# Layer 0's scores of batches 2 to 7: four heads in one block on TensorE, the second pair of heads in two other PSUM banks

## What is computed

```python
gk = k.reshape(B, G, KV_HEADS, N, D_HEAD).mean(axis=1)
gv = v.reshape(B, G, KV_HEADS, N, D_HEAD).mean(axis=1)
scores = jnp.einsum('bghnd,bhsd->bhns', gq, gk)
scores = scores + gbias
attn = jax.nn.softmax(scores.astype(jnp.float32), axis=-1)
out = jnp.einsum('bhns,bhsd->bhnd', attn, gv)
```

## Time and profile before

| what | value |
|---|---|
| three executions | 761.25, 761.84 (median), 762.82 us |
| the profiled execution | 761.44 us |
| its span, first to last instruction | 759.5 us |
| PE busy | 738.1 us, 97% of the span |
| DVE busy | 555.8 us, 73% |
| ACT busy | 383.1 us, 50% |
| POOL busy | 187.2 us, 25% |
| TensorE clock granted, mean | 0.998 of full speed |

### The profile page before, as it was taken

The page is one execution under the profiler, slowest core; times in us unless marked ns, Lnnn a source line. Parts: engine busy times, 40 slices in busy tenths (PEclk is TensorE's granted clock), DMA queues, the critical chain, the costliest instruction groups (busy, mean ns, idle before and its releaser), DMA issues.

```text
span 759.5 us, 16816 instructions
## 1 busy us (share of the span) xinstructions
PE 738.1 (97%) x6559; PEld 556.0 (73%) x6559; DVE 555.8 (73%) x1642; ACT 383.1 (50%) x1063; POOL 187.2 (25%) x235
## 2 busy tenths in 40 slices
PE   7899999999999999999999999999998999999996
PEld 5565757775787578657865786588576878999996
DVE  4878875869776877688678867787859764255997
ACT  3755557356535654555456545642561436554422
POOL 0235212153116311540154025304210422000000
PEclk9999999999999999999999999999999999999999
DMA  7950020402040204020402030213204304000000
GB/s 226 377 142 1 4 82 2 111 1 58 3 111 1 58 2 112 2 56 7 109 1 57 19 96 6 53 31 83 57 2 107 118 3 111 1 1 1 15 22 22
DMA packets 55702, 43.07 MB, mean 57 GB/s; under 512 B 37900, under 2 KB 48804, under 8 KB 54216
## 3 DMA queue, kind: packets, MB, share of 16 engines
q1 hardware_dynamic: 55624, 42.01, 20.8%
HBM read 32.42 MB, written 9.58 MB: 55 GB/s over the span
## 4 chain that ended last, share of the span: by engine, by line
PE 83%; DVE 11%; ACT 2%; DMA 1%; issue 1%; POOL 1%; SPq 0%; DVEq 0%; ACTq 0%
PE ps L1753 15%; PE ps L1836 14%; PE ps L1896 7%; PE ps L2059 4%; PE ps L2037 4%; PE ps L1739 4%; PE ps L2006 4%; PE ps L1761 4%; PE ps L1787 3%; PE ps L1848 3%; PE ps L1774 3%; DVE shared L1482 2%; DVE shared L1475 2%; PE ps L1703 2%; PE ps L1919 2%; PE ps L1931 2%
## 5 line engine op out<-in xcount | busy, mean ns | idle before, releaser
L1753 PE MATMUL ps<-veF,hB 128*128 128x512 f32 x256 | 121.6, 606 | 0.0
L1301 DVE COPY_PREDICATED shared<-ghot,ps 128x512 f32<-128x512 int32 x128 | 88.2, 727 | 3.4 <-PE ps L1753 0.6
L848 ACT ACTIVATE sc<-sc,nmax 128x128 f32<-128x128 f32 (+1 forms) x128 | 57.1, 447 | 58.4 <-DVE nmax L1287 58.4
L1753 PEld LDWEIGHTS ps<-veF,hB 128*128 128x128 f32 x256 | 45.2, 189 | 49.4 <-issue 40.2
L648 POOL TENSOR_TENSOR sc<-sc,rg 128x384 f32<-128x384 f32 x64 | 51.6, 827 | 70.0 <-DVE rg L1274 70.0
L1836 PE MATMUL ps<-early_masks,oeF 128*128 128x256 f32 x256 | 63.5, 386 | 2.7 <-DVE wide L1331 1.6
L705 POOL TENSOR_TENSOR ve<-mv,eps 128x2 f32<-128x2 f32 x24 | 8.6, 357 | 233.3 <-DVE mv L1187 233.3
L1836 PE MATMUL ps<-wide,oeF 128*128 128x256 f32 x256 | 62.3, 386 | 0.0
L1896 PE MATMUL ps<-hC,early 128*64 128x128 f32 x1024 | 61.7, 275 | 0.2
L2037 PE MATMUL ps<-hE,veF 128*128 128x256 f32 x256 | 59.5, 382 | 0.3 <-ACT wide L957 0.3
L1896 PEld LDWEIGHTS ps<-hC,early 128*64 128x64 f32 x1024 | 55.7, 137 | 5.4 <-ACT wide L886 2.5
(11 more groups left out here) (253 smaller groups left out, 1527.5 us busy)
## 6 DMA issues: line engine op xcount, KB each, us to landing
chosen<-hot_scratch SPq DMA_DIRECT2D x16, 512.0 KB, 5.8
v_scratch<-shared SPq DMA_DIRECT2D x16, 512.0 KB, 5.3
vg<-v_scratch SPq DMA_DIRECT2D x16, 512.0 KB, 5.4
veF<-in_L_ffn_value_experts SPq DMA_DIRECT2D x1, 2048.0 KB, 9.9
oeF<-in_L_ffn_output_experts SPq DMA_DIRECT2D x1, 2048.0 KB, 16.0
early<-in_L_attn_w_qkv SPq DMA_DIRECT2D x1, 1536.0 KB, 16.6
shared<-bias_scratch SPq DMA_DIRECT2D x2, 512.0 KB, 6.2
veF<-in_L_ffn_W SPq DMA_DIRECT2D x1, 1024.0 KB, 5.3
```

The costliest lines, as they stand in the source:

```text
L848: act.activation(v, v, ACT.Exp, bias=nmax[:, h % RING, t:t + 1], scale=-1.0, accum_out=denB[:, h * T + t:h * T + t + 1]).then_inc(s_("f_e" ...
L1301: dve.copy_predicated(val[:, t, :].rearrange("p (h k) -> p h k", h=HF), ghot[:, t * HF:(t + 1) * HF, e].bitcast(I32).unsqueeze(2) .broadca ...
L1753: pe.matmul(ps[:, vbank(j), :], tok(hB, t), veF[:, :].rearrange("p (h e k) -> p e h k", h=HF, e=EF)[:, e, :, :], start=True, stop=True).th ...
```

## The change

For batches 2 to 7 PE now makes the scores of all four heads at place 1, directly behind chunk 1 of the products, in one block of eight matmuls. The first pair stays in banks 4 and 6, the second goes to banks 7 and 1. The wait for DVE's reading of the first pair (`a_sc`) is gone; each pair still raises `a_s`. The turned scores, until now in banks 1 and 2, go to banks 2 and 4. The code of DVE, ACT and POOL stands in the same order as before, DVE's S1 still at place 4; only the bank numbers in it differ. Batches 0 and 1 are as they were.

```diff
         def logits_bank0(b, p, hp):
             if b == 1 and p == 1:
                 return 1 + hp
-            return (4 + p if early_batch(b) else 4) + 2 * hp
+            if early_batch(b):
+                return 4 + p + 2 * hp
+            return ((4, 6), (7, 1))[p][hp]
 
         def turned_bank0(b, hp):
-            return 5 + 2 * hp if early_batch(b) else 1 + hp
+            return 5 + 2 * hp if early_batch(b) else 2 + 2 * hp
...
-                if n in (S0, S1):
-                    p = (S0, S1).index(n)
-                    if p == 0:
+                if n == S0 or n == S1 and early_batch(b):
+                    if n == S0:
                         wait_apart(pe, (s_("a_qs"), b + 1), (s_("a_ks"), b + 1))
...
-                    elif not early_batch(b):
-                        pe.wait_ge(s_("a_sc"), b * 8 + 4)
-                    for t in range(T):
-                        for hp in range(2):
-                            mm = pe.matmul(ps[:, logits_bank0(b, p, hp), t * N:(t + 1) * N],
-                                           qT[head_rows(hp), p, t * P:(t + 1) * P], kT[head_rows(hp), p, :],
-                                           start=True, stop=True)
-                    mm.then_inc(s_("a_s"), 1)
+
+                    for p in ((S0, S1).index(n),) if early_batch(b) else range(2):
+                        for t in range(T):
+                            for hp in range(2):
+                                mm = pe.matmul(ps[:, logits_bank0(b, p, hp), t * N:(t + 1) * N],
+                                               qT[head_rows(hp), p, t * P:(t + 1) * P], kT[head_rows(hp), p, :],
+                                               start=True, stop=True)
+                        mm.then_inc(s_("a_s"), 1)
```

## The result

The changed kernel is slower. Its median is 762.51 us (12 runs, 761.62 to 763.35) beside 761.55 us for the kernel before (12 runs, 759.95 to 762.82): ratio 1.0017, 95% interval 1.0009 to 1.0024, so 0.7 to 1.8 us more time (the two medians by themselves are 0.96 us apart). The forecast was 2.1 us less.

A forecast was written before the change was run, and what follows sets the result against it. PE was taken as the bound; gains of 0.16 (batch 2), 0.39 (batch 3) and 4 x 0.38 (batches 4 to 7) sum to 2.07 us, giving 759.8 us, own range 759.2 to 760.4, full range 758.8 to 761.8.

The forecast's parts named there:

- What bounds the kernel, and the join: PE bounds batches 3 to 7; joining two blocks of four score matmuls saves 0.39 us of PE's time a batch.
- The estimate of 0.33: Score blocks: two drains of TensorE less a batch, worth 0.33 us by the skill's page; the prediction stayed with the rows.
- Batch 2: At T0 the removed wait comes back as one for POOL; of 1.00 us gain, 0.16 is left.
- the 1 us that I had named as a sign: Batch 2: about 1 us of PE's idle time before or within T0, for POOL's line 640.
- Batch 3: No tail of layer 1 beside it, POOL's division just in time for T0: gain 0.39 us.
- DVE's S1 and the norm behind it: Batches 4 to 7: S1 and the normed tile come 0.38 us earlier, PE's wait stays: gain 0.38 each.
- The rival "slower": Batches 4 to 7: chunk 3's delay makes the normed tile 0.87 us later; 2.9 us slower, 764.8; chance 0.06.
- The sign that I named for being wrong: At PE's turning of the normed tile, a wait of over 0.5 us would show the forecast wrong.
- the rival before it: The wait moves to T0 everywhere, PE standing still for POOL's division; about 761.6 us, chance 0.07.

The follow-up runs named there:

- e4_before_pool_more: The kernel before, with one more POOL operation (128x512) behind the two divisions of N0 in batches 4 to 7; 764.13 us, ratio 1.0039.

## Why the prediction was wrong

**What bounds the kernel, and the join.** Right. PE's own work was the bound; the block of eight cost 0.87 more than a block of four, 0.39 less than two, in the chain at batch 6 (16 records in 2.00 us, as in batch 0), with the banks 7 and 1 as with batch 0's. The estimate of 0.33 from the Trainium skill's "TensorE: Matmul & The Clock Gate", "Single matmul latency", was low; by batch 3's segment it is 0.40.

**Batch 2.** Right: 0.13 us left of 1.00, forecast 0.16. The removed wait came back as one for POOL's division, in two pieces. The records show 0.51 us of it as idle time, half of the 1 us that I had named as a sign; by the starts 0.87 us came back:

```profile
84.59 0.66 PE L1693 MATMUL ps<-ident,sc 128*128 128x128 f32 x4 [0.17 <-POOL sc L642]
...
85.59 0.66 PE L1693 MATMUL ps<-ident,sc 128*128 128x128 f32 x4 [0.34 <-POOL sc L642]
```

**Batch 3.** Right: 0.40, forecast 0.39.

**DVE's S1 and the norm behind it.** This step failed. It read: "it begins straight after the reciprocal ... 373.80, 0.38 earlier. Behind it in DVE's order stand mask 12 ... the tile 0.38 earlier: the wait stays about what it is." The start of S1 was right: the reciprocal at 373.89 and S1 at 373.98 in a trace that runs 0.18 us later. But the prediction took mask 12's length as fixed, a term that it put at nothing without a reason. It let POOL divide until 376.01 in one paragraph, and moved S1 and with it mask 12 forward in the next, which puts the mask at 375.56 - 0.38 = 375.18. It asked of POOL only who waits for it (rightly no one: T0 began 0.40 us earlier, without a wait), not what runs beside it. Measured from the batch's first score matmul, mask 12 began 0.41 us earlier and took 0.71 us longer, so the addition, the tile and PE's turning of it came 0.30 us later. Each batch lost 0.30 instead of gaining 0.38: 4 x 0.68 = 2.7 us, the term that turned the sign. From -2.07 this gives +0.65. The interval is +0.7 to +1.8, so between nothing and a microsecond more stays unexplained, as in e4_before_pool_more.

**The rival "slower"** had the right victim, the normed tile and PE's wait for it, and the wrong cause and price: it wanted S1 later than 374.18, S1 was earlier (373.98), and it was slower all the same, by about 1 us and not 2.9. Its chance of 0.06 stood for the wrong mechanism, so that "slower" came out is no credit to it. The sign that I named for being wrong (a wait of over 0.5 us at the turned tile) did just show, with 0.51. (A slip in the rival before it changes nothing: 761.84 less batch 2's 0.16 is 761.7, not 761.6.)

**The trace of before had it.** All masks of the kernel before, by the source view of line 1331 (duration ns: min/median/max):

```profile
L1331 DVE TENSOR_TENSOR early_masks<-chosen,oT x64: 657/685/2379, 72.3 to 586.6; 128x512 f32<-128x512 uint8 x64
L1331 DVE TENSOR_TENSOR wide<-chosen,oT x64: 657/685/1391, 77.6 to 590.0; 128x512 f32<-128x512 uint8 x64
```

The longest of the second row stands in batch 2 behind S1, in a run of four masks that takes 3.20 us from 85.25, beside the division of the earlier trace rows that ends at 86.09. The 2379 stands beside POOL here, and PE waited for that very mask:

```profile
71.74 1.90 POOL L606 TENSOR_TENSOR vg<-x,mv 128x1024 f32<-128x1024 f32 x1
73.78 2.16 POOL L609 TENSOR_TENSOR vg<-vg,rstd 128x1024 f32<-128x1024 f32 x1
...
72.28 4.21 DVE L1331 TENSOR_TENSOR early_masks<-chosen,oT 128x512 f32<-128x512 uint8 x2
...
76.54 1.13 PE L1836 MATMUL ps<-early_masks,oeF 128*128 128x256 f32 x4 [1.11 <-DVE early_masks L1331]
```

The two masks end at 76.49, again 0.55 us after POOL (73.78 + 2.16 = 75.94). This is the other row, the 1.1 us that I passed over: PE lost time to the same overlap in the kernel before. A maximum of two and of three times the median was the question to ask. I had written of batch 2 only that DVE is late.

## What to carry to other kernels

When work moves on one engine, lay the new times of all engines over each other, not only the waits between them: an operation on POOL that nobody waits for can still stretch one on DVE that everybody waits for. Before trusting a duration in a sum, look at its maximum beside its median, and find what ran beside the longest. When a block is joined on the bound engine, look for the step that now has the least slack; here moving one short reciprocal into DVE's idle time turned +0.17% into -0.35%, and with the scores beside it -0.48%.

## What the runs showed of the hardware

A mask, a DVE operation with two inputs in SBUF, does not do its work beside a POOL operation that reads SBUF. It starts in the records, and ends 0.54 to 0.55 us after POOL's does. That holds for every mask of over 0.72 us in all eight traces, whatever it overlapped: 0.79 us where POOL's operation had begun 0.80 us ahead of it, 1.12 at 0.47 ahead, 1.40 at 0.19 ahead, 2.38 beside the longer operation of line 609. So the mask waits for POOL's end, and is not merely slower. The whole length counts as busy time, and no view of waits shows it.

It goes the other way too. In the norm behind mask 12 two tiny operations of POOL come up while masks 13 and 14 run (changed kernel, batch 6):

```profile
377.71 1.26 DVE L1333 TENSOR_TENSOR wide<-chosen,oT 128x512 f32<-128x512 uint8 x2
377.87 0.55 POOL L707 TENSOR_TENSOR ve<-mv,eps 128x2 f32<-128x2 f32 x1 [1.70 <-DVE mv L1189]
378.50 1.03 POOL L709 TENSOR_TENSOR rstd<-ve,half 128x2 f32<-128x2 f32 x1
```

Their usual lengths are 0.20 and 0.70 us (medians of 24 each). The 0.68 us more stand on the way to the normed tile in batches 4 to 7, before the change as after it. No run here takes them away.

Operations of DVE of other kinds ran beside POOL at their usual time, in the changed kernel: the scores' pass with one input in PSUM (line 1218, max 426 ns for a median of 419; 27 of 64 beside POOL), the predicated copy out of PSUM (56 of 128), and the reduction with one SBUF input (29 of 32):

```profile
L1218 DVE CUSTOM_DVE_ANT_0 sc<-ps,early x64: 387/419/426, 18.8 to 450.1; 128x256 f32<-128x256 f32 x64
...
L1303 DVE COPY_PREDICATED shared<-ghot,ps x128: 703/729/743, 46.9 to 554.6; 128x512 f32<-128x512 int32 x128
...
L1390 DVE TENSOR_REDUCE max<-wide x32: 649/677/686, 154.2 to 624.5; 128x8 f32<-128x512 f32 x32
```

But the plain multiplication by a scalar from SBUF to SBUF is held up with one input: line 1229 of the kernel before, in the attention of batches 0 and 1, beside POOL's division of the other head. Three of its eight are 1.23 us long and end 0.15 us after POOL.

```profile
L1229 DVE TENSOR_SCALAR sc<-sc,rdenA x8: 341/352/1233, 23.0 to 36.3; 128x256 f32<-128x256 f32 x8
```

The Trainium skill has a rule for this, on the page "SBUF — State Buffer", section "SBUF: two separate sides": DVE and GpSimd share a pair of SBUF ports under an exclusive lock, taken for a whole instruction by whichever starts first, and it counts for DVE operations in a two-port mode, and for those with two SBUF inputs against a GpSimd operation that reads SBUF. The masks of all eight traces agree, and so do the two POOL operations above. Which of the two started first can't be told from the records to the last 0.05 us: the long ones of line 1229 are recorded 0.04 us ahead of POOL's operation, and were held up all the same. By that rule, which I had not weighed, mask 12 would stand until POOL's instruction ends. As an estimate from the prediction's 376.01 and a mask's 0.69 us, it would end at 376.70, where it had ended at 376.24 before, and the forecast's sum would have had the right sign.
